# Log-sum over nodes of |d| read from the score's bank, fold moved directly behind R's products, zero products redistributed

## The reference, cut to what matters

```python
def step(carry, ht):                      # 256 steps, one after the other
    H_prev, H_prev_tilde = carry          # windows of the last 5 items, (8, 5, 128)
    temp = tanh(H_prev @ W1 + (ht @ W2)[:, None, :] + H_prev_tilde @ W3)
    w_t = softmax(temp @ v, axis=1)       # over the 5 items
    ht_hat = sum(H_prev_tilde * w_t, axis=1)
    ht_tilde = ht + relu(ht_hat)
    # both windows are shifted by one item: ht and ht_tilde go in
...
t = t + recurrence(layer_norm(t))
t = t + experts(layer_norm(t))            # gelu(x @ W1 + b1) @ W2 + b2, two of eight
```

## Time and profile before

| | us |
|---|---|
| median of 3 runs | 577.03 |
| lowest, highest | 575.26, 580.84 |
| the profiled execution's own time | 582.32 |
| its span (first to last instruction) | 580.4 |

### The profile page before, as it was taken

How to read it: one execution, slowest core, us unless ns; L and a number is a source line. 1 busy time by engine, 2 the same in 40 slices (tenths; PEclk the granted TensorE clock), 3 DMA queues, 4 the chain that set the end, 5 groups by cost and what they waited for, 6 DMA issues and landing times. The chain is left out here.

```text
span 580.4 us, 19441 instructions
## 1 busy us (share of the span) xinstructions
PE 557.9 (96%) x6331; PEld 446.0 (77%) x6331; DVE 413.3 (71%) x2867; ACT 354.0 (61%) x1440; POOL 47.4 (8%) x101
## 2 busy tenths in 40 slices
PE   6999879999999999999999999999999999999987
PEld 3555436778888888888888888888888888888875
DVE  2456555777777878787877787878787877777763
ACT  2335645556666666666666666666666666666654
POOL 1000000010101010101010101010101010101010
PEclk9555569999999999999999999999999999999999
DMA  8000000000000000000000000000000000000000
GB/s 228 17 2 1 0 0 3 2 3 2 3 6 3 6 3 7 3 7 3 6 3 6 3 6 3 7 3 7 2 6 3 6 3 7 2 7 3 8 2 10
DMA packets 7507, 5.84 MB, mean 10 GB/s; under 512 B 1216, under 2 KB 6896, under 8 KB 7408
## 3 DMA queue, kind: packets, MB, share of 16 engines
q1 hardware_dynamic: 6784, 4.57, 2.8%
q10 hardware_dynamic: 528, 0.03, 0.1%
q0 software_dynamic: 96, 0.00, 0.0%
HBM read 3.55 MB, written 1.05 MB: 8 GB/s over the span
## 5 line engine op out<-in xcount | busy, mean ns | idle before, releaser
L470 ACT ACTIVATE th<-bank 128x32 f32<-128x32 f32 x255 | 51.3, 201 | 145.4 <-PE bank L696 145.4
L938 DVE TENSOR_TENSOR_SCAN CC<-th,DE 128x16 f32<-128x16 f32 x510 | 115.3, 226 | 0.5 <-issue 0.5
L728 PE MATMUL bank<-f,hid 128*128 128x128 f32 x512 | 112.9, 302 | 1.0 <-ACT hid L492 0.6
L497 ACT ACTIVATE GF<-Z,cst 64x32 f32<-64x32 f32 x255 | 105.4, 413 | 11.7 <-DVE Z L989 2.5
L942 DVE SCALAR_TENSOR_TENSOR DE<-CC,yh 128x40 f32<-128x40 f32 x509 | 81.9, 203 | 27.2 <-DVE yh L1005 0.5
L938 DVE TENSOR_TENSOR_SCAN C<-th,DE 128x16 f16<-128x16 f32 x255 | 49.3, 193 | 73.0 <-ACT th L470 68.3
L633 PE MATMUL bank<-xnT,f1p 128*128 128x128 f16 x1024 | 99.2, 219 | 0.2 <-ACT hid L492 0.2
L696 PE MATMUL bank<-Tf,v 128*128 128x32 f32 x510 | 99.3, 277 | 0.0
L685 PE MATMUL bank<-Tf,nv 128*128 128x32 f32 x510 | 98.9, 276 | 0.0
L492 ACT ACTIVATE hid<-bank,b1T 128x128 f32<-128x128 f32 x256 | 94.4, 369 | 5.7 <-PE bank L633 4.8
L694 PE MATMUL bank<-GF,cst 128*128 128x32 f32 x510 | 95.3, 269 | 0.0
(11 more groups left out here) (135 smaller groups left out, 827.3 us busy)
## 6 DMA issues: line engine op xcount, KB each, us to landing
x_tok<-in_x_dram SPq DMA_DIRECT2D x4, 256.0 KB, 4.3
f<-in_L_ffn_W_dram SPq DMA_DIRECT2D x1, 1024.0 KB
out_dram<-acc SPq DMA_DIRECT2D x16, 64.0 KB
w<-in_L_attn_W_dram SPq DMA_DIRECT2D x3, 64.0 KB, 3.9
cst<-shape_constants_dram SPq DMA_DIRECT2D x1, 148.5 KB, 2.5
wfg<-in_L_conv_Wf_dram ACTq DMA_DIRECT2D x1, 8.0 KB, 2.3
wfg<-in_L_conv_Wg_dram ACTq DMA_DIRECT2D x1, 8.0 KB, 2.3
bhc<-in_L_conv_bh_dram POOLq DMA_DIRECT2D x1, 0.1 KB, 3.4
```

What stands on the lines that cost most here:

```text
L470: act.activation(th[p][:, 0:W4, 1], psS[p][:, 0:W4], ACT.Tanh, bias=-K0 / 2, scale=0.5 / WS).then_inc(th_ready, 1)
L497: act.activation(GF[p][0:NODES, :], Z[p][0:NODES, :], ACT.Tanh, bias=half_nodes, scale=half_nodes).then_inc(f_ready, 1)
L728: mm = pe.matmul(psO[e % 2][:, 0:D], hid[u % 2][:, :], f2[:, u, :], start=(half == 0), stop=(half == HH - 1))
L938: return dve.tensor_tensor_scan(flat[0], flat[1], flat[2], 0.0, ALU.mult, ALU.add)
```

## The change

The nodes are no longer geometric but those of a logistic function: 56 of 64 have an offset t = log(1 + exp(u)) and a weight, each eighth one has a large offset and a weight that takes off what the seven before it owe. The node tanh is taken of (|d| + t) / 2, where |d| is the absolute value of the score's difference. ScalarE takes it from the bank with an Abs into a new tile `A` (64 partitions, 24 columns), so the scale of the node tanh is a constant and only its bias is a per-partition operand; it works on 24 columns instead of 32. The constant K0 leaves the biases of th and Relu. The last 8 columns of `GF` are constants, set once. Z leaves VectorE. The node tanh stands behind the Abs, ahead of the unit's gelu. On TensorE the fold stands directly behind R's products, ahead of the h products; the zero product of each step is gone; a step without a unit has five zero products instead of four, and step `LEAD` of tile 1 has three more. The first node tanh, ahead of the first step, is replaced by a copy of constants, and four memsets go.

```diff
-            act.wait_ge(z_ready, 1)
-            act.wait_ge(g_ready, 1)
-            act.activation(GF[1][0:NODES, :], Z[1][0:NODES, :], ACT.Tanh, bias=half_nodes, scale=half_nodes).then_inc(f_ready, 1)
...
                     if chain and not first:
                         act.wait_ge(score_ready, n)
-                        act.activation(th[p][:, 0:W4, 1], psS[p][:, 0:W4], ACT.Tanh, bias=-K0 / 2, scale=0.5 / WS
+                        act.activation(th[p][:, 0:W4, 1], psS[p][:, 0:W4], ACT.Tanh, scale=0.5 / WS
                                        ).then_inc(th_ready, 1)
-                        act.activation(GF[p][:, 0:W4 - B], psS[p][:, B:W4], ACT.Relu, bias=K0 * WS, scale=-1.0
-                                       ).then_inc(g_ready, 1)
+                        act.activation(GF[p][:, 0:W4 - B], psS[p][:, B:W4], ACT.Relu, scale=-1.0)
+                        act.activation(A[p][:, :], psS[p][0:NODES, B:W4], ACT.Abs).then_inc(a_ready, 1)
+                        act.wait_ge(a_ready, n)
+                        act.activation(GF[p][0:NODES, 0:W4 - B], A[p][:, :], ACT.Tanh, bias=half_nodes, scale=0.5 / WS
+                                       ).then_inc(f_ready, 1)
...
-                    if chain and not first:
-                        act.wait_ge(z_ready, n + 1)
-                        act.wait_ge(g_ready, n + 1)
-                        act.activation(GF[p][0:NODES, :], Z[p][0:NODES, :], ACT.Tanh, bias=half_nodes, scale=half_nodes).then_inc(f_ready, 1)
...
                         product(in5(psA[p][:, 0:W5]), w3w, relu, False, True, ALL_PRODUCTS[2:]).then_inc(projected, 1)
-                        h_products(k, i, q)
-                        keep_busy(psS[p], 256, 1)
-
-                        pe.wait_ge(g_ready, n)
                         pe.wait_ge(f_ready, n)
                         pe.matmul(psS[p][:, 0:W4], fold_w, GF[1 - p][:, :], start=False, stop=False)
+                        h_products(k, i, q)
+
                         pe.wait_ge(tf_ready, n + 1)
...
                     if chain and not first and not unit:
-                        keep_busy(psA[q], 256, 4)
+                        keep_busy(psA[q], 256, 5)
+                    if k == 1 and i == LEAD:
+                        keep_busy(psA[q], 256, 3)
...
-            dve.tensor_copy(GF[1][:, :], g_init).then_inc(g_ready, 1)
+            dve.tensor_copy(GF[0][:, :], g_init).then_inc(init, 1)
+            dve.tensor_copy(GF[1][:, :], g_init).then_inc(f_ready, 1)
...
-                        dve.scalar_tensor_tensor(Z[p][:, 0:W4 - B], th[p][:, B:W4, 1], -1.0,
-                                                 th[p][:, B:W4, 1], ALU.mult, ALU.max).then_inc(z_ready, 1)
```

More of the change, by code:

```diff
@@ L63 @@
 LIN = NODES
-NODE_H = (np.log(22.0) - np.log(1e-8)) / (NODES - 1)
+RUN = 8
+SPREAD = 19.0
 def node_constants():
-    a = np.exp(np.log(1e-8) + NODE_H * np.arange(NODES)).astype(np.float32)
-    h = np.float32(NODE_H)
-    return a, h, float(np.sum(float(h) * np.tanh(a.astype(np.float64))))
+    u = np.linspace(-SPREAD, SPREAD, NODES - NODES // RUN)
+    h = u[1] - u[0]
+    t = np.full(NODES, 80.0)
+    w = np.zeros(NODES, np.float32)
+    owed = 0.0
+    at = 0
+    for j in range(NODES):
+        if j % RUN < RUN - 1:
+            t[j] = np.log1p(np.exp(u[at]))
+            w[j] = WS * h / 2 / (1 + np.exp(-u[at]))
+            owed += float(w[j])
+            at += 1
+        else:
+            w[j] = -owed
+            owed += float(w[j])
+    return t, w
 def shape_constants():
-    a, h, _ = node_constants()
+    t, w = node_constants()
     c = np.zeros((P, 2 * P + 1 + E + W4), np.float32)
@@ L79, in shape_constants @@
     c[LIN, P:2 * P] = -1.0
-    c[0:NODES, P:2 * P] = h * np.float32(WS)
-    c[0:NODES, 2 * P] = a / 2
+    c[0:NODES, P:2 * P] = w[:, None]
+    c[0:NODES, 2 * P] = t / 2
     c[:, 2 * P + 1:2 * P + 1 + E] = np.arange(E)
@@ L84, in shape_constants @@
         c[:, 2 * P + 1 + E + j * B:2 * P + 1 + E + (j + 1) * B] = np.log(OLD - j) * WS
+    c[0:NODES, 2 * P + 1 + E:] = 1.0
     return c
 def build(nc, x, Wf, bf, Wg, bg, Wh, bh, Wv, bv, gamma, v, W1, W2, W3, Wr, br, F1, b1, F2, b2, consts, out):
-    K0 = node_constants()[2]
     x_tok_dram = x.rearrange("b h w c -> b (h w) c").rearrange("b (u p) c -> p (b u) c", p=P)
@@ L170, in build @@
         GF = pair("GF", [P, W4])
-        Z = pair("Z", [P, W4])
+        A = pair("A", [NODES, W4 - B])
         DE = pair("DE", [P, W5, 2])
@@ L239, in build @@
         crit_ready = sem("crit_ready")
-        z_ready = sem("z_ready")
+        a_ready = sem("a_ready")
         r1_ready = sem("r1_ready")
         r2_ready = sem("r2_ready")
-        g_ready = sem("g_ready")
         f_ready = sem("f_ready")
@@ L834, in initial_state @@
                     dve.memset(CC[q][:, :, :], 0.0).then_inc(init, 1)
-                    dve.memset(GF[q][:, :], 0.0).then_inc(init, 1)
-                    dve.memset(Z[q][:, :], 1.0).then_inc(z_ready if q == 1 else init, 1)
                 dve.memset(C16[0][:, :, :], 0.0).then_inc(r1_ready, 1)
@@ L867, in _ @@
                     initial_state()
-            dve.wait_ge(init, 9)
-            dve.tensor_copy(GF[1][:, :], g_init).then_inc(g_ready, 1)
+            dve.wait_ge(init, 6)
+            dve.tensor_copy(GF[0][:, :], g_init).then_inc(init, 1)
+            dve.tensor_copy(GF[1][:, :], g_init).then_inc(f_ready, 1)
             dve.wait_ge(ht_done, B)
```

## The result

The changed kernel takes 691.3 us (median of 4 runs, 680.4 to 733.5), the kernel before 578.9 (575.3 to 583.5) on the same chip. The ratio is 1.179, with a 95% interval of 1.162 to 1.196: slower by 18%, where 557.4 was forecast, with a range of 548 to 571. The profiled execution took 680.35 us, with a span of 678.4.

The account below looks back on a forecast made before the run. The prediction took the node tanh's chain, ending last by about 0.09 us a step, as the bound. 239 x 0.09 = 21.5 us, less 0.9, 0.4 and 0.6, gave 19.6: 577.0 to 557.4 us, range 548 to 571.

Parts of the forecast that it names:

- Zeros: Zero products on TensorE: one removed per step, five instead of four without a unit, three more at LEAD; all costed at 0.
- The fallen clock: Rival: TensorE's clock falls as unit steps lose a 256-column product; 0.8 us per slow step, 660 us, chance 0.10.
- the b2 step: Step 13 of a tile, where the b2 product delays C's and R's products; forecast to stay at 2.04 us, gaining nothing.
- the thin step at 131 to 134 us: One step with neither zeros nor a down product; the clock stayed full there in the trace before the change.
- The bound: Step time: th, scans, Z, node tanh, fold, v's product ends last, by about 0.09 us of the 1.82 us step.
- Node tanh: New route on ScalarE: start at T+0.40 (T is th's start) instead of T+0.62, length 320 ns, bounds 277 and 414.
- Fold moved: On TensorE, fold directly behind R's products at T+0.81, PE free for v at T+1.18; step 1.73 instead of 1.82 us.
- Z at zero: Taking Z off VectorE's queue, between CC and R, gains zero; bounds 0 and 0.03 us.
- Gelu: ScalarE gelu behind the node tanh: covered, except 0.9 us lost over step 1 of the tiles and 0.4 at the end.
- Sum: Whole kernel: 239 x 0.09 = 21.5 us, less 0.9, 0.4 and 0.6, gives 19.6 us gain and 557.4 us.

## Why the prediction was wrong

The step that failed is the one under Zeros: "that is PE time nobody waited for. ... I cost all of them at 0". The time of that product was indeed waited for by nobody. But its work held TensorE's clock, and it was the cover of everything else in the sum. The cost appeared in another place, as the price of 128 steps at half clock. The fallen clock was among the rivals, at 0.10, with its price at 0.8 us a step (measured 0.91, 1.12 in steps 0, 3 and 11, and 1.42 in the b2 step, 3.47 against 2.05) and 660 us for half of the steps at the low clock. The profiled run had that half and took 680. What was wrong was its chance, and a range that left it out. The reason I gave against it, the thin step at 131 to 134 us in which the clock stayed full, was a single step; without its extra zeros it holds in the new kernel too. The weak place was not there, but the b2 step, which I had priced as a step that "gains nothing" and not looked at as a place where the clock could fall. That it falls there is shown; why it does, whether for the eight-row passes or for the step's length, is open. The earlier trace rows also showed that PE's busy share is no sign: 3.40 of 3.40 us ahead of the fall at 15.2, as 3.48 of 3.50 here.

The rest, by its own steps:

- *The bound.* Right. The node tanh's chain ended last by 0.09; with it early, the step is 1.72 to 1.73, forecast 1.73.
- *Node tanh.* Start T+0.37 for T+0.40 forecast, since Abs follows Relu by 0.07 and the wait on its own engine costs 0.03 (301.90 to 301.93). Length 314 ns for 320.
- *Fold moved.* It follows R's products at T+0.81, as forecast. But its place brings nothing, which the forecast didn't say; v is free at T+1.28 in either order.
- *Z at zero.* Right for the plain step. Step 10 of a tile came down more than others, from 1.86 to 1.73, and stays at 1.73 with Z put back, so it wasn't Z. The traces show what made R late there before: VectorE's first scan took 0.226 us in 14 of 15 steps 10, against 0.192 in their neighbours and in the steps 10 of the kernel with the zero at its old place, and R started at T+0.58. Why the scan was longer is open.
- *Gelu.* Step 1 loses nothing in the median: it takes 1.72 us like the others.
- *Sum.* 22.7 us from the first th to the last with the clock held, forecast 20.0 for that part (19.6 and the 0.4 behind the last step). The step gains 0.095 instead of 0.09, which is 1.2 us, and steps 1 and 10 give most of the rest. With the zero back at its old place the kernel takes 554.1, where 557.4 had been forecast for the change.
- *Where the 680 come from.* 444.8 us of steps at full clock, plus what 128 steps at half clock lose: 24 steps with a transpose (0, 3 and 11) 1.12 each, 8 b2 steps 1.42, 8 steps with the gate's products (5) 0.97, the other 88 0.91. That is 444.8 + 26.9 + 11.4 + 7.8 + 80.1 = 571; the trace has 570.3 from the first th (86.3) to the last (656.6).

The version that beats both is the change with the zero kept ahead of v's product: 554.1 us, or 552.4 without the three zeros of the one thin step; these two can't be told apart, since both recurrences take 444.7 to 444.8 us. Times of the kernels in which the clock holds differ by 10 us and more, from 549.3 to 562.9, through the stage ahead of the recurrence, where the clock is up or down by turns: the first th comes at 81.6 us in one profiled run and at 93.4 in another.

## What to carry to other kernels

A filler product is no idle work if it holds TensorE's clock: before taking one out, go through the steps one by one, and not by their mean. Here the longest step and its neighbours decided, and three zeros of sixteen were enough. A busy share near 100% in the profile didn't show it. And when a change shortens a step, try the fillers apart from the rest: here the edit that was worth 23 us and the edit that cost 137 were in the same diff, and the second hid the first.

## What the hardware showed that was not expected

- The clock didn't recover by work of the same kind. In the changed kernel TensorE was busy for 344.60 of 344.60 us at half clock (312.0 to 656.6); it came back at 661.8, in the tail, where only unit and down products are left.
- A longer step can bring the clock down with no product taken out. The kernel before with its fold moved has the same products in a step of 1.99 us instead of 1.82, with PE idle for 0.28 instead of 0.08, and lost the clock in the fifth step in the profiled run; the four runs took 803 to 808 us.
- The Trainium skill (TensorE: Matmul & The Clock Gate, section HAM oscillation) puts the rule as one against idle gaps of PE. These traces differ: in the changed kernel PE has 0.02 us idle in the 3.50 ahead of the fall, by the profile. The measurement decides, with the reserve that the profile models the ends of products.
- Whether it falls at a given b2 step varies: the changed kernel passed those of tiles 1 to 6 and fell in tile 7 in one run, and four runs took 680, 685, 697 and 734 us; the kernel without zeros near b2 got through all of them in one run of four (549.5 us).
